# A bank for the last value rows, and low parts ahead of maxima, in a fused attention and feed-forward kernel

## What is computed

```python
def block(x, ctx):
    n = layernorm(x)                       # over the 512 columns
    q, k, v = n @ Wq, ctx @ Wk, ctx @ Wv   # 8 heads of 64
    a = softmax(q k^T / 8) v               # 512 queries x 77 keys per batch and head
    x = x + a @ Wo + bo
    n2 = layernorm(x)
    xq = int8-like rounding of n2, one scale for the whole tensor
    h = silu(xq @ wg^T) * (xq @ wu^T)      # 1408 wide, weights rounded row by row
    return x + (h rounded the same way, one scale) @ wd^T
```

## Time and profile before

| | us |
|---|---|
| median of 3 executions | 543.21 (542.95 to 543.4) |
| the profiled execution | 542.76 |
| its span, first to last instruction | 540.8 |
| TensorE busy | 526.9 (97%) |
| VectorE busy | 472.8 (87%) |
| ScalarE busy | 294.8 (55%) |
| GpSimd busy | 231.8 (43%) |

### The profile page before, as it was taken

How to read it: one execution, slowest core, us unless ns; L and a number is a source line. 1 busy time by engine, 2 the same in 40 slices (tenths; PEclk the granted TensorE clock), 3 DMA queues, 4 the chain that set the end, 5 groups by cost and what they waited for, 6 DMA issues and landing times.

```text
span 540.8 us, 8058 instructions
## 1 busy us (share of the span) xinstructions
PE 526.9 (97%) x2733; PEld 356.2 (66%) x2740; DVE 472.8 (87%) x879; ACT 294.8 (55%) x414; POOL 231.8 (43%) x349
## 2 busy tenths in 40 slices
PE   8999899999999999999999899999999999999997
PEld 7878688887888878888778644444444445444444
DVE  4967898989989899898989789999999988899784
ACT  4843655555455654554444546555555643999500
POOL 4397759589596886856454000000000000055442
PEclk9999999999999999999999999999999999999999
DMA  8819366856667565434959955941342120399977
GB/s 313 282 78 307 100 170 199 263 151 209 193 225 244 170 223 182 155 116 166 218 91 324 273 141 213 330 118 21 98 118 66 52 39 28 121 326 226 157 105 129
DMA packets 82942, 93.83 MB, mean 173 GB/s; under 512 B 47085, under 2 KB 50157, under 8 KB 82645
## 3 DMA queue, kind: packets, MB, share of 16 engines
q1 hardware_dynamic: 77877, 84.13, 50.6%
q0 software_dynamic: 4320, 7.87, 9.2%
q10 hardware_dynamic: 704, 1.31, 0.7%
HBM read 47.51 MB, written 37.78 MB: 158 GB/s over the span
## 4 chain that ended last, share of the span: by engine, by line
PE 81%; DVE 11%; issue 2%; POOL 2%; DMA 2%; ACT 1%; ACTq 0%; DVEq 0%; POOLq 0%
PE QO L570 14%; PE SP L575 14%; PE QO L306 5%; PE QO L308 5%; PE QO L307 5%; PE SP L371 5%; PE PTP L622 4%; PE QO L622 3%; PE SP L622 3%; PE MI L444 2%; PE MI L442 2%; PE MI L443 2%; PE PTP L404 2%; PE WOP L622 2%; PE WOP L444 2%
## 5 line engine op out<-in xcount | busy, mean ns | idle before, releaser
L1491 POOL DMA_DIRECT2D out<-n2b x30 | 30.3, 1044 | 206.6 <-DVE n2b L1304 206.6
L854 ACT ACTIVATE sil<-QO,fsc 128x512 f32<-128x512 f32 x87 | 59.7, 687 | 70.1 <-PE QO L570 68.4
L570 PE MATMUL QO<-nT,wgu 128*128 128x512 bf16 x340 | 87.3, 379 | 0.1
L575 PE MATMUL SP<-nT,wgu 128*128 128x512 bf16 x340 | 87.3, 379 | 0.0
L1241 DVE SCALAR_TENSOR_TENSOR h<-SP,fsc,sil 128x512 f32<-128x512 f32 x87 | 65.1, 748 | 8.3 <-PE SP L575 6.2
L1395 POOL TENSOR_TENSOR PN<-P,rs 128x512 f32<-128x512 f32 x64 | 44.2, 711 | 47.7 <-DVE rs L937 47.7
L1247 DVE TENSOR_REDUCE hmx<-h 128x1 f32<-128x512 f32 (+1 forms) x89 | 60.1, 680 | 2.9
L575 PEld LDWEIGHTS SP<-nT,wgu 128*128 128x128 bf16 x340 | 33.2, 98 | 40.2 <-DVE h L1241 0.3
L570 PEld LDWEIGHTS QO<-nT,wgu 128*128 128x128 bf16 x340 | 33.0, 98 | 40.4 <-DMA nT<-qb 0.7
L684 ACT ACTIVATE P<-P,r 128x616 f32<-128x616 f32 x32 | 25.9, 811 | 58.8 <-DVE P L928 58.8
L306 PE MATMUL QO<-xTs,wqs 128*128 128x512 f32 x124 | 50.3, 406 | 2.1 <-DVE xTs L892 1.9
(11 more groups left out here) (223 smaller groups left out, 1201.6 us busy)
## 6 DMA issues: line engine op xcount, KB each, us to landing
xTr<-in_xT SPq DMA_DIRECT2D x8, 1024.0 KB, 7.4
xn<-in_x SPq DMA_DIRECT2D x32, 256.0 KB, 4.0
out<-x SPq DMA_DIRECT2D x32, 256.0 KB, 3.0
n_rows<-n SPq DMA_DIRECT2D x32, 256.0 KB, 2.6
n2b<-n_rows SPq DMA_DIRECT2D x32, 256.0 KB, 3.7
out<-n2b POOLq DMA_DIRECT2D x30, 256.0 KB, 6.5
h_spill<-h SPq DMA_DIRECT2D x2, 2816.0 KB, 9.2
h<-h_spill SPq DMA_DIRECT2D x6, 768.0 KB, 7.2
```

The lines of the kernel that those rows point to most:

```text
L570: mm = e.matmul(QO[:, at:at + 512], wgu_v[:, k, cols(ic)], nT[:, b % 2, :, k, :], start=(k == 0), stop=(k == 3))
L575: mm = e.matmul(SP[:, at:at + 512], wgu_v[:, k, cols(NI + ic)], nT[:, b % 2, :, k, :], start=(k == 0), stop=(k == 3))
L854: e.activation(sil[:, n % SR, :], QO[:, (n % 2) * 512:(n % 2) * 512 + 512], ACT.Silu, scale=fsc[:, ic:ic + 1]).then_inc(silu, 1)
```

## The change

- **v rows 4** are computed in bank MI (`v_bank`), leave `QO_USES`, and stand on TensorE behind chunk 0 of batch 2, PT(3) ahead of it. wo(1), the first to use MI after it, waits for its low part.
- **K**: eight of the nine matmuls of bank 7 stand ahead of the wait for the last low part of Wk, the ninth with its siblings of the other banks.
- **q_ahead(b)** takes the place of `q_chunk(b, 0)` for b from 1: all eight matmuls on high parts of x^T first, each step waiting for its high chunk, then the four on low parts, each waiting for its own (`LO_ORDER`).
- **VectorE**: PT_low(3) ahead of the maxima of tile 4, v_low(4) behind its sums; in the first pass the statistics of tiles 6 and 7 and the maxima of weight 3 move from ahead of PV_low(0) to behind PT_low(4) and behind the sums of tile 5.
- **ScalarE**: q_copy(2,0) and soft_exp(4) ahead of v_high(4); w_round(2) behind PV_high(0), w_round(3) behind q_copy(2,1); in every pass q_copy(b+2,0) ahead of w_round(s+2) and normed(s-3).
- **GpSimd**: low chunk 3 of batch 1 behind soft_norm(0); the statistics of tiles 6 and 7 behind soft_norm(5).

```diff
@@ -209,6 +209,9 @@
+        def v_bank(r):
+            return MI[:, :] if r == 4 else qo_bank("v", r)
         def S_bank(n):
@@ -230,7 +233,7 @@
         QO_USES = [("q", 0, m) for m in range(4)] + [("v", r) for r in range(4)]
-        QO_USES += [("q", 1, m) for m in range(4)] + [("v", 4), ("q", 2, 0)]
+        QO_USES += [("q", 1, m) for m in range(4)] + [("q", 2, 0)]
         for b_ in range(6):
@@ -254,6 +257,9 @@
             LO_POOL[b_], LO_DVE[b_] = (0, 1, 2), (3,)
+        LO_ORDER = {1: (0, 1, 2, 3), **{b_: (0, 2, 1, 3) if b_ == 2 else (0, 1, 2, 3) for b_ in range(2, NB)}}
@@ -323,8 +329,15 @@
                     k_part(m, k, 2)
+                if k == 2:
+                    w.wait_ge(wq_c, 4)
+                    for k0 in range(2):
+                        for i in (0, 2, 1):
+                            k_part(7, k0, i)
+                    k_part(7, 2, 0)
+                    k_part(7, 2, 2)
                 w.wait_ge(wk_lo, k + 1)
-                for m in range(7):
+                for m in range(8 if k == 2 else 7):
                     mm = k_part(m, k, 1)
@@ -356,12 +369,27 @@
+            def q_ahead(b):
+                bank, pairs = qo_bank("q", b, 0), q_pairs(0)
+                wait_qo_free(w, "q", b, 0)
+                for k in range(4):
+                    w.wait_ge(xT_hi, 4 * b + k + 1)
+                    e.matmul(bank, pairs[k][0], pairs[k][2], start=(k == 0), stop=False)
+                    e.matmul(bank, pairs[k][1], pairs[k][2], start=False, stop=False)
+                for k in LO_ORDER[b]:
+                    w.wait_ge(xT_lo_pool, lo_pool_count(b - 1) + sum(i <= k for i in LO_POOL[b]))
+                    w.wait_ge(xT_lo_dve, lo_dve_count(b - 1) + sum(i <= k for i in LO_DVE[b]))
+                    mm = e.matmul(bank, pairs[k][0], pairs[k][3], start=False, stop=(k == LO_ORDER[b][-1]))
+                mm.then_inc(q_mm, 1)
             def v_rows(r):
...
                 ws = slice(r * 128, r * 128 + n)
-                wait_qo_free(w, "v", r)
+                if r < 4:
+                    wait_qo_free(w, "v", r)
                 w.wait_ge(wv_lo, 3)
-                three(qo_bank("v", r)[0:n, :], [(cts[:, 0, k, ws], cts[:, 1, k, ws], wvs[:, 0, k, :], wvs[:, 1, k, :])
+                three(v_bank(r)[0:n, :], [(cts[:, 0, k, ws], cts[:, 1, k, ws], wvs[:, 0, k, :], wvs[:, 1, k, :])
                                                 for k in range(3)]).then_inc(v_mm, 1)
@@ -433,6 +461,8 @@
                     w.wait_ge(PT_lo, 32)
+                elif n == 1:
+                    w.wait_ge(v_lo, 5)
                 elif n == 31:
@@ -458,11 +488,6 @@
             k_chunk(2)
-            w.wait_ge(wq_c, 4)
-            for k in range(3):
-                for i in (0, 2, 1):
-                    mm = k_part(7, k, i)
-            mm.then_inc(k_mm, 1)
             q_first()
@@ -475,7 +500,7 @@
             v_rows(3)
-            q_chunk(1, 0)
+            q_ahead(1)
             S(2)
@@ -484,9 +509,9 @@
             S(4)
+            PT(3)
+            q_ahead(2)
             v_rows(4)
-            PT(3)
-            q_chunk(2, 0)
             for b in range(1, 7):
@@ -507,7 +532,7 @@
                 if b + 2 < NB:
-                    q_chunk(b + 2, 0)
+                    q_ahead(b + 2)
             wo(23)
@@ -676,7 +701,7 @@
                 w.wait_ge(st_v[r % 2], 16 * (r // 2))
-                copy(vst[0:n, r % 2, 0, :], qo_bank("v", r)[0:n, :]).then_inc(v_hi, 1)
+                copy(vst[0:n, r % 2, 0, :], v_bank(r)[0:n, :]).then_inc(v_hi, 1)
@@ -764,11 +789,10 @@
             w_round(1)
+            PT_high(3)
+            q_copy(2, 0)
+            soft_exp(4)
             v_high(4)
-            PT_high(3)
-            soft_exp(4)
-            q_copy(2, 0)
-            w_round(2)
             for b in range(1, 7):
@@ -776,10 +800,12 @@
                 if b == 1:
-                    w_round(s - 1)
+                    w_round(2)
                 PT_high(s)
...
                 q_copy(b + 1, 1)
+                if b == 1:
+                    w_round(3)
                 soft_exp(s + 2)
@@ -797,11 +823,11 @@
                 PT_high(s + 3)
+                if b + 2 < NB:
+                    q_copy(b + 2, 0)
                 if s + 2 < 26:
...
                 normed(s - 3)
-                if b + 2 < NB:
-                    q_copy(b + 2, 0)
             normed(22)
@@ -912,7 +938,7 @@
                 w.wait_ge(st_v[r % 2], 16 * (r // 2))
-                less(vst[0:n, r % 2, 1, :], qo_bank("v", r)[0:n, :], vst[0:n, r % 2, 0, :]).then_inc(v_lo, 1)
+                less(vst[0:n, r % 2, 1, :], v_bank(r)[0:n, :], vst[0:n, r % 2, 0, :]).then_inc(v_lo, 1)
@@ -1065,25 +1091,23 @@
             split_lo(2, 3)
+            PT_low(3)
             soft_max(4)
-            v_low(4)
             soft_sub(4)
-            PT_low(3)
             soft_sum(4)
             soft_rec(4)
+            v_low(4)
             w_top(2)
...
             w_inverse(2)
-            first_stats(6)
-            first_aggr(6)
             for b in range(1, 7):
                 s = 4 * b
-                first_stats(s + 3)
-                w_top(s - 1)
-                first_aggr(s + 3)
-                w_scale(s - 1)
-                w_inverse(s - 1)
                 if b > 1:
+                    first_stats(s + 3)
+                    w_top(s - 1)
+                    first_aggr(s + 3)
+                    w_scale(s - 1)
+                    w_inverse(s - 1)
                     residual(s - 5)
@@ -1093,8 +1117,17 @@
                 PT_low(s)
+                if b == 1:
+                    first_stats(6)
+                    first_aggr(6)
                 soft_sum(s + 1)
                 soft_rec(s + 1)
+                if b == 1:
+                    first_stats(7)
+                    w_top(3)
+                    first_aggr(7)
+                    w_scale(3)
+                    w_inverse(3)
                 for t in (1, 2):
@@ -1368,8 +1401,8 @@
-            def split_lo(b):
-                for k in LO_POOL[b]:
+            def split_lo(b, *chunks):
+                for k in chunks or LO_POOL[b]:
                     w.wait_ge(xT_hi, 4 * b + k + 1)
@@ -1433,10 +1466,11 @@
             e.memset(PN[:, :, 512:640], 0.0).then_inc(const, 1)
-            split_lo(1)
+            split_lo(1, 1)
...
             soft_norm(0)
+            split_lo(1, 3)
             first_scale(3)
@@ -1453,14 +1487,16 @@
             w_integer(2)
-            first_scale(6)
-            first_bias(6)
             for b in range(1, 7):
                 s = 4 * b
-                first_scale(s + 3)
                 if b > 1:
+                    first_scale(s + 3)
                     second_scale(s - 5)
                 soft_norm(s + 1)
+                if b == 1:
+                    first_scale(6)
+                    first_bias(6)
+                    first_scale(7)
                 w_integer(s - 1)
```

## The result

The changed kernel takes 547.58 us (median of 5 runs, 546.36 to 548.12); the kernel before took 543.21 us in the same comparison (5 runs, 542.92 to 544.36). The ratio is 1.0075, with a 95% interval of 1.0064 to 1.0085. The forecast was 539.0 us: the sign was wrong. It is the fastest of the five. The other four took 546.96 to 548.12 us at a mean granted clock of 0.994, so part of what separates the medians is not in this trace.

A forecast was written before the change was run, and what follows sets the result against it. TensorE, busy 97% of 540.8 us, was taken as the bound. Terms 2.45 - 0.40 - 0.15 + 2.33 = 4.2 us gained brought the median from 543.21 to 539.0 us, range 537.9 to 541.3.

The forecast's parts named there:

- Step 1: Start: eight bank 7 matmuls fill the wait for Wk's low part, bringing q_first's fourth step 0.31 us earlier.
- Step 2: Batch 1's first transpose: soft_norm(0) no longer waits behind low chunk 3, the hole closes; gain so far 1.25 us.
- Step 3: From S(4) to the first output product, which starts at 63.6 instead of 65.81: 2.21 us gained.
- The new stall at PT(3): TensorE idles 1.4 us before PT(3), a stall that the v rows used to hide.
- my bounds: VectorE's two splits beside GpSimd: from 0.68 us each, leaving 63.6 as it is, to 3.9 together, costing 0.8.
- Step 4: Scores of tile 5: with VectorE's statistics moved later, S(5) starts at 67.91 instead of 70.36, gain 2.45 us.
- Step 5: Work moved behind S(5): 0.40 us lost at S(7), 0.15 at S(9), nothing from weight loads or GpSimd.
- rival (e): SP's queue delays load_w(5), so w_top(5) and PT(7) wait and the kernel is slower: 544.3 us, chance 0.04.
- Step 6: Loop: q_ahead removes five stalls before the next batch's chunk 0, gaining 2.33 us.
- rival (b): The loop gives nothing: its wait returns before PV_all or S because VectorE sets the pace; 541.3 us, chance 0.10.

The follow-up runs named there:

- e_w0_early: a_os_apart with the load of weight 0 issued on SP ahead of five loads of input tiles: 543.44 us, 1.0003 of the kernel before.
- a_os_apart: Changed kernel with os_ moved off vst's bytes, the wait for the stores moved to the buffer now there: 543.68 us, 0.9999 of the kernel before.
- f_v4_back: Changed kernel with v rows 4 alone put back in their old place, bank MI kept, os_ still on vst: 545.21 us, 1.0031 of the kernel before.
- f_v4_stats_back: f_v4_back with statistics 6 and 7, w_top(3), w_round(2) and GpSimd's scales also in the old order: 543.49 us, 1.0007 of the kernel before.
- e_w2_back: a_os_apart with w_round(2) alone put back ahead of PV_high(0) on ScalarE: 544.70 us, 1.0035 of the kernel before.
- b_loop_q: Kernel before with q_ahead for chunk 0 of batches 3 to 7 alone: 542.95 us, 0.9989 of the kernel before.
- b_loop_q_copy: b_loop_q with q_copy(b+2,0) also ahead of w_round and normed on ScalarE: 542.71 us, 0.9984 of the kernel before.
- the reliefs: GpSimd's bias add, VectorE's maximum, or both cut to 8 of 512 columns in a_os_apart: 542.74, 541.40, 540.07 us; both in the kernel before: 541.71.
- g_chunk: f_v4_stats_back with batch 2's query chunk 0 in the old form instead of q_ahead(2): 543.07 us, 0.9995 of the kernel before.
- g_chunk_os: g_chunk with os_ laid apart from vst: 543.76 us, 0.9994 of the kernel before.

## Why the prediction was wrong

**Step 1, K part 7: half of 0.31 us, and none of it in this trace.** q_first starts at 19.02 us, as I had it, but its fourth step at 21.43, where I had 21.18, and S(0) no earlier than before. TensorE in the changed kernel, then in the kernel before:

```profile
21.43 0.47 PE L357 MATMUL QO<-xTs,wqs 128*128 128x512 f32 x1
...
30.36 1.38 PE L399 MATMUL SP<-kst,qs 128*128 128x154 f32 x8
```

```profile
30.34 1.38 PE L371 MATMUL SP<-kst,qs 128*128 128x154 f32 x8
```

I took VectorE's last low part for fixed at 20.45 us. It starts there at 20.61 in the changed kernel, and between 20.24 and 20.64 over all traces. Counted from that start, S(0) stands 9.75 to 9.80 us behind it in the fourteen traces with the edit and 9.89 to 9.93 in the five without, so the edit is worth 0.1 to 0.2 us.

**Step 2, first transpose: the hole closed, the carry-over failed.** The transpose comes 0.91 us earlier, without a wait, and not 1.25: the 0.31 of step 1 are missing. I let all of batch 0's end move with TensorE, to S(4) 1.25 us earlier; it moved 0.38. The failing assumption was that all inputs come from TensorE. One comes from a DMA: VectorE's w_top(0), waiting for weight 0 (2.90 us, where it waited 1.34 before), with the sums, the subtraction, the exponentials and the query copies behind it. e_w0_early shows it: S(4) 0.66 earlier.

**Step 3, the first output product: half of the term.** 1.10 us instead of 2.21; of the shortfall of 1.11, 0.87 is there already at S(4). The new stall at PT(3) was forecast at 1.4 us and is 1.26. The splits took 2.96 us where I took 2.45, inside my bounds, and still covered by TensorE's work.

**Step 4, scores of tile 5: this is the step that failed.** "S(5) starts at 67.91: gain 2.45 us." It starts at 72.15. I took VectorE's statistics for the last thing that S(5) waits for, and after their removal went on to the next thing in VectorE's queue. I did not read what ScalarE's os copy waits for in the program: the stores of value rows, whose source os_ overlaps. The trace of before could not show that wait, since the store at 63.17 had landed before it was needed; the line in the program could. The prediction follows the stores and loads that stand behind weight 2; v rows 4's own store is in none of its sums. a_os_apart prices it at 3.9 us of 547.58 by the medians and at 3.0 by the starts of S(5) in the two traces. Without the wait the step's own arithmetic holds: in a_os_apart S(5) starts at 69.14, 4.29 us behind the first output product, where I had 4.31 (67.91 less 63.6).

**Step 5, what is late next.** From S(5) to S(7) the changed kernel loses 0.33 us and a_os_apart 0.26; the forecast was 0.40. S(9) waits 1.4 where I had 0.15: that is the term that was mis-sized. I followed VectorE and SP, and took GpSimd's two us of delay for harmless because its splits for batch 3 were in time. It was the second norm's scale, further down the same queue, that was late: GpSimd, ScalarE's normed, w_round, os copies, S(9). f_v4_back against f_v4_stats_back shows the cause (1.35 us of wait against none), and the medians stand 1.7 us apart. The SP queue of rival (e) was late in the changed kernel (load_w(5) at 85.53 against 80.46 in the earlier trace rows), and VectorE did wait for it:

```profile
88.38 0.69 DVE L1010 TENSOR_REDUCE wmx<-wraw 128x1 f32<-128x512 f32 x1 [1.13 <-DMA wraw<-in_ffn_w_gate]
```

But it did not decide. PT(7) started 0.2 us late by the distance to the matmul ahead of it, and in e_w2_back VectorE's wait is gone and S(9) waits all the same.

**Step 6, the loop: rival (b).** Worth 2.33 us by my sum, 0.3 and 0.6 by b_loop_q and b_loop_q_copy, none in the changed kernel. I had argued that VectorE's idle time per pass is several times 0.55 us. That idle time is not in the place where the slack is needed. The work of VectorE and of GpSimd holds the passes too, which the reliefs show: 32.7 us with both loads in place, 32.2 with both relieved.

The rivals: (b) came true for its part; (e) had the right sign and the wrong queue. The wait that decided, a store's landing through shared bytes, was in no rival. Rival (e) has a slip as well: by its own rule, one for one past 84.9, a landing at 91.5 gives 545.6 us; the 544.3 belongs to 90.2.

f_v4_stats_back, with neither the store's wait nor the one before S(9), is no faster than before in the median. The fall of the clock accounts for 1.3 us in its trace, by the 5.83 us from the first output product to S(5) against 4.55 before, and all twelve of its executions had a mean clock of 0.997 or less. The executions of g_chunk and g_chunk_os without a fall, 0.7 us faster than the kernel before, point the same way. What stays open is why the rest of the 4.2 us does not come even there, and when the clock falls. No version that does all the work beats the kernel before by more than 0.2% in the median; b_loop_q_copy is best at 0.9984.

## What to carry to other kernels

Before a write is moved later, list in the program who waits for everything that it triggers, its stores too, and look for buffers laid over its source: such a wait is invisible in the old trace as long as it is met, and shows as "issue" in the new one. When TensorE is busy 97% of the time, relieve each other engine by an instruction or two that is simply left out, before any reordering: if the gaps of TensorE move but the pass keeps its length, a second chain holds it. Small idle stretches gathered into one need not cost the same as the small ones: here the granted clock fell behind the one. Compare the granted clock of every execution, not of the profiled one alone.
